# A first group that begins with its first tile: two sets of four PSUM banks, an earlier first weight piece, and a third context block turned inside head six

## The reference, cut to what matters

```python
    x = x + _L0_xattn_ref(ctx_2048, ctx_2048, _layernorm(x, axis=-1), L0_xattn_ssm_kernel, L0_xattn_D, 8)
    x = x + _L0_ffn_ref(_layernorm(x, axis=-1), L0_ffn_gate_w, L0_ffn_w_gate, L0_ffn_w_up, L0_ffn_w_down, L0_ffn_sw_gate, L0_ffn_sw_up, L0_ffn_sw_down)
    # _L0_xattn_ref
        kv = jnp.einsum('bhil,bhjl->bijhl', k_, v_)
        kv_f = jnp.fft.rfft(kv, n=fft_size)
        kernel_f = jnp.fft.rfft(ssm_kernel, n=fft_size)
        y = jnp.fft.irfft(kv_f * kernel_f, n=fft_size)[..., :L]
        out = y + kv * D[None, None, None, :, None]
        out = jnp.einsum('bijhl,bhil->bjhl', out, q_)
    # _L0_ffn_ref
        scores = jax.nn.softmax(x @ gate_w.T, axis=-1)
        topk_w, topk_i = jax.lax.top_k(scores, K)
        gact = jax.nn.silu(jnp.einsum('ech,ehi->eci', xg, w_gate))
        mid = gact * jnp.einsum('ech,ehi->eci', xg, w_up)
        eout = jnp.einsum('eci,eih->ech', mid, w_down) * wbuf[..., None]
        shared = jax.nn.silu(x @ sw_gate) * (x @ sw_up) @ sw_down
```

## Time and profile before

| | |
|---|---|
| median of 3 runs | 613.25 us (612.37 to 613.38) |
| the profiled execution | 613.41 us, span 611.3 us |
| PE busy | 591.2 us, 97% of the span |
| DVE, ACT, POOL busy | 485.8, 289.7, 407.4 us |
| mean granted TensorE clock | 0.994 |

### The profile page before, as it was taken

How to read it: one execution, slowest core, us unless ns; L and a number is a source line. 1 busy time by engine, 2 the same in 40 slices (tenths; PEclk the granted TensorE clock), 3 DMA queues, 4 the chain that set the end, 5 groups by cost and what they waited for, 6 DMA issues and landing times.

```text
span 611.3 us, 13710 instructions
## 1 busy us (share of the span) xinstructions
PE 591.2 (97%) x4411; PEld 552.7 (90%) x4411; DVE 485.8 (79%) x1279; ACT 289.7 (47%) x520; POOL 407.4 (67%) x499
## 2 busy tenths in 40 slices
PE   7989999999999999999999999999999999999993
PEld 7768989999999989999999898999999999999992
DVE  6999787679779689598699879999878888877730
ACT  3426334434435334345261344576556665656631
POOL 6988798778888789789771272187448886334242
PEclk9999999999999999999999999999999999999997
DMA  6665315226236145251340147698888889888443
GB/s 178 233 184 173 105 36 173 73 74 166 88 94 165 49 111 155 52 142 47 86 113 2 53 160 240 200 291 229 226 215 242 228 224 236 240 234 245 123 59 45
DMA packets 60238, 91.50 MB, mean 150 GB/s; under 512 B 4262, under 2 KB 36006, under 8 KB 60188
## 3 DMA queue, kind: packets, MB, share of 16 engines
q1 hardware_dynamic: 52912, 74.00, 39.9%
q0 software_dynamic: 7168, 16.78, 13.4%
q10 hardware_dynamic: 108, 0.08, 0.1%
HBM read 73.76 MB, written 17.09 MB: 149 GB/s over the span
## 4 chain that ended last, share of the span: by engine, by line
PE 82%; DVE 6%; POOL 4%; issue 4%; ACT 2%; DMA 1%; DVEq 1%; POOLq 0%; ACTq 0%
PE gu L684 19%; PE gu L843 14%; PE yb L562 11%; PE mb L860 10%; PE yb L843 7%; PE gu L722 7%; PE mb L534 4%; PE yb L614 3%; PE yb L534 2%; POOL kv L1257 1%; DVE prod L1521 1%; PE gu L763 1%; DVE prod L1523 1%; DVE oT L1541 1%; DMA xg<-normalised_tokens,slot_rows 1%
## 5 line engine op out<-in xcount | busy, mean ns | idle before, releaser
L684 PE MATMUL gu<-xT,sw 128*128 128x256 f32 (+2 forms) x1104 | 136.4, 281 | 0.0
L684 PEld LDWEIGHTS gu<-xT,sw 128*128 128x128 f32 (+2 forms) x1104 | 131.8, 180 | 0.5 <-issue 0.2
L1257 POOL TENSOR_TENSOR kv<-kT 128x256 f32 (+3 forms) x232 | 106.1, 496 | 0.0
L1274 POOL TENSOR_TENSOR kvl<-kv,kvh 128x1440 fp32r<-128x1440 f32 (+1 forms) x26 | 82.3, 3167 | 26.3 <-ACT kvh L971 26.0
L1521 DVE TENSOR_TENSOR prod<-yb,qT 128x64 f32<-128x64 f32 (+10 forms) x272 | 74.7, 285 | 17.4 <-PE yb L614 11.7
L1541 DVE TENSOR_REDUCE oT<-prod 128x256 f32<-128x2048 f32 x32 | 73.0, 2280 | 0.1
L971 ACT ACTIVATE kvh<-kv 128x1440 fp32r<-128x1440 f32 (+1 forms) x26 | 35.2, 1352 | 73.9 <-POOL kv L1264 37.4
L562 PE MATMUL yb<-kvh,tlast 128*128 128x288 f32 x280 | 66.1, 297 | 0.0
L1523 DVE TENSOR_TENSOR prod<-yb,qT 128x96 f32<-128x96 f32 (+10 forms) x238 | 64.2, 270 | 0.0
L860 PE MATMUL mb<-ed,midh 128*128 128x512 f32 x180 | 57.4, 400 | 0.0
L1817 DVE TENSOR_TENSOR ew<-raw_w,ew 128x704 fp32r<-128x704 f32 x64 | 55.1, 882 | 0.3 <-ACT ew L1119 0.3
(11 more groups left out here) (218 smaller groups left out, 1296.0 us busy)
## 6 DMA issues: line engine op xcount, KB each, us to landing
raw_w<-in_L_ffn_w_gate_dram SPq DMA_DIRECT2D x16, 704.0 KB, 7.0
raw_w<-in_L_ffn_w_up_dram SPq DMA_DIRECT2D x16, 704.0 KB, 8.6
raw_d<-in_L_ffn_w_down_dram SPq DMA_DIRECT2D x16, 512.0 KB, 4.3
tlast<-toeplitz_taps SPq DMA_DIRECT2D x20, 384.0 KB, 3.7
tstep<-tap_steps SPq DMA_DIRECT2D x20, 256.0 KB, 4.2
c_t<-in_ctx_dram SPq DMA_DIRECT2D x16, 256.0 KB, 5.3
x_t<-in_x_dram SPq DMA_DIRECT2D x16, 256.0 KB, 5.1
normalised_tokens<-xn SPq DMA_DIRECT2D x16, 256.0 KB, 2.9
```

Source lines behind the costliest of these rows:

```text
L684: last = pe.matmul(bank[0:m, u * GT:(u + 1) * GT], sw[:, c, a, col:col + m], xT[:, c, b, :], start=(c == 0 and (a, b) == PASSES[0]), stop= ...
L1257: last = pool.tensor_tensor(to[:, :, POFF[d]:POFF[d] + w], src[:, :, 0:w], src[:, :, d * B:HD * B], ALU.mult)
L1274: pool.tensor_tensor(kvl[:, s, 0:nb, :], kv[:, s, 0:nb, :], kvh[:, s, 0:nb, :].bitcast(fp32), ALU.subtract)\
```

## The change

- **First group by tiles.** The first context tile and the first x tile are loaded ahead of the second ones, with a semaphore each (`ctx_first`, `x_first`). Tile 0 is turned, normalised and multiplied first (`first_stats`, `inverse_tile`); heads 0 and 1 use tile 0 alone. The second queries are turned inside head 2 (`second_queries`). PE begins with 2 dummy products instead of 5, and has 5 and 1 later instead of 17.
- **Banks.** `gu` and `mb` become one tensor `other` of four banks. Heads 1 and 3 go to `other`, heads 0, 2 and 4 to `yb`. DVE multiplies heads 1, 2 and 4 whole instead of by halves.
- **Taps.** `tap_rows` is loaded by SP, `skip_t` is ACT's first transfer, SP stores `first_taps`. The split of the taps (`padhl`) and the tap steps (`steps_of`, `stephl`) move behind the first products on DVE; the rounding of `stephl` goes to ACT and its subtraction to POOL.
- **Weights.** ACT rounds piece 0 ahead of the second copied queries. POOL's order becomes piece 0, `stephl`, `pairs(4)`, `inverse_x(1)`, piece 2, `pairs(5)`, piece 1, `inverse_t(0)`, piece 3.
- **Head five.** The third context block (`prep_ctx(2)`) is turned in the middle of `convolve(5)`, into `gu`, ahead of group 0's normalised tokens, which go into `gu` too.

```diff
+        other = es.enter_context(nc.psum_tensor("other", [P, LB, 512], fp32))
+        gu, mb = other[:, 0:2, :], other[:, 2:LB, :]
...
-        BY_HALVES = (0, 1, 2, GH, GH + 1)
-        FIRST_POOL = 3
+        BY_HALVES = (0, GH + 1)
+        FIRST_POOL = 4
...
+        FIRST_HOMES = {1: ((other, 0), (other, 2)), 3: ((other, 0), (other, 2)), GH + 1: ((mb, 0), (yb, 0))}
...
# SP
-            load_group(0, parts="c")
-            load_group(0, parts="x")
-            sp.dma_start(gate_rows[:], gate_w).then_inc(gate_in, 16)
+            sp.dma_start(tap_rows[:], taps).then_inc(taps_in, 16)
+            sp.dma_start(c_t[:, 0, :], c_g[0, 0]).then_inc(ctx_first[0], 16)
+            sp.wait_ge(pad_whole, 1)
+            sp.dma_start(first_dram, pad[0:WHOLE, :]).then_inc(first_out, 16)
+            sp.dma_start(c_t[:, 1, :], c_g[0, 1]).then_inc(ctx_first[1], 16)
             sp.wait_ge(first_out, 16)
             load_first(0)
-            load_group(1, parts="x")
+            sp.dma_start(x_t[:, 0, 1, :], x_g[0, 1]).then_inc(x_first[1], 16)
             load_first(1)
             load_first(2)
+            sp.wait_ge(c_tr, TT)
+            load_group(1, parts="c")
             load_first(3)
+            load_group(1, parts="x")
...
# PE
+                    convolve(GH * g, 0)
+                    pe.wait_ge(d_mul, 4)
+                    prep_q(g)
+                    mixed_out(g - 1, g)
+
+                    def turn():
+                        prep_ctx(g + 1)
+                        pe.wait_ge(k_ev, TT * (g + 2))
+                        normalised(g - 1)
+
+                    convolve(GH * g + 1, 1, turn)
...
-            idle_products(5)
-            prep_ctx(0)
-            idle_products(17)
-            convolve(0, 0, {1: lambda: prep_q(0)})
+            idle_products(2)
+            prep_ctx(0, [0])
+            idle_products(5)
+            gate_turned()
+            prep_ctx(0, [1])
+            idle_products(1)
+            prep_q(0, [0])
+            convolve(0, 0)
+            convolve(1, 1)
...
+            convolve(2, 2, {LB - 1: second_queries})
             prep_ctx(1)
...
# POOL
             pairs(1, 0, 1)
+            inverse_tile(1, x_stat, x_pow, x_rs)
             pairs(2, 0, 2)
             pairs(3, 0, 3)
+            split_shared(0)
+            pool.wait_ge(steps_h, 1)
+            pool.tensor_tensor(stephl[:, 1, :, :], steps_of[:], stephl[:, 0, :, :].bitcast(fp32), ALU.subtract)\
+                .then_inc(steps_hl, 1)
             pairs(GH, 1, 0)
             inverse_x(1)
+            split_shared(2)
             pairs(GH + 1, 1, 1)
-            split_shared(0)
-            split_shared(2)
             split_shared(1)
+            inverse_t(0)
             first_steps()
...
# DVE
+            gate_low()
+            multiply(0, 0, 0, lambda: first_stats(1, x_stat))
+            add_up(0, 0, 0)
             prep_stats(1, [0])
-            multiply(0, 0, 0, lambda: prep_stats(1, [1]))
-            add_up(0, 0, 0)
             head(1, 0, 1)
-            gate_low()
+            prep_stats(1, [1])
             head(2, 0, 2)
```

More of the change, by code:

```diff
@@ L616, in convolve, with prep_ctx, prep_q @@
                 last.then_inc(conv, 1)
[L618 to L621, removed]
+            def prep_ctx(g, tiles=range(TT)):
+                if isinstance(g, int) and g == 0:
+                    pe.wait_ge(ctx_first[tiles[0]], 16)
+                else:
+                    pe.wait_ge(ctx_in, 32 * g)
+                if isinstance(g, int) and g == 2:
+                    pe.wait_ge(x1_ok, TT)
+                else:
+                    wait(pe, n_l, TT * (g - 1))
+                for t in tiles:
                     wait(pe, q_ev, TT * (g - 1) + t + 1)
-                    transposes(mb[:, t, :], lambda c: c_t[:, t, c * P:(c + 1) * P]).then_inc(c_tr, 1)
-            def prep_q(g):
+                    bank = gu if isinstance(g, int) and g == 2 else mb
+                    transposes(bank[:, t, :], lambda c: c_t[:, t, c * P:(c + 1) * P]).then_inc(c_tr, 1)
+            def prep_q(g, tiles=range(TT)):
                 wait(pe, lg_ok, g - 1)
-                for t in range(TT):
+                for t in tiles:
                     pe.wait_ge(x_nrm, TT * g + t + 1)
@@ L635, in mixed_out @@
                     pe.wait_ge(d_sum, GH * g + (t + 1) * GH // TT)
-                    last = transposes(mb[:, t, :], lambda c: oT[:, LB - 1 - c, t * P:(t + 1) * P])
+                    if isinstance(g, int) and g == 0:
+                        pe.wait_ge(d_mul, 4)
+                    last = transposes(turned(g)[:, t, :], lambda c: oT[:, LB - 1 - c, t * P:(t + 1) * P])
                     last.then_inc(o_tr, 1)
@@ L942, in norm_q @@
             def norm_q(g, tiles=range(TT)):
-                act.wait_ge(x_rs, g + 1)
+                if isinstance(g, int) and g == 0 and tiles[0] == 0:
+                    act.wait_ge(tile_rs, 1)
+                else:
+                    act.wait_ge(x_rs, g + 1)
                 for t in tiles:
@@ L961, in evacuate @@
                     tile = dst[:, bass.ds(g % 2, 1), :, t * P:(t + 1) * P].rearrange("p s c w -> p (s c) w")
-                    act.activation(tile, mb[:, t, :].rearrange("p (c w) -> p c w", c=LB), ACT.Copy).then_inc(signal, 1)
+                    bank = gu if isinstance(g, int) and g == 2 and dst is kT else mb
+                    act.activation(tile, bank[:, t, :].rearrange("p (c w) -> p c w", c=LB), ACT.Copy).then_inc(signal, 1)
             def round_kv(n, s):
@@ L1302, in first_steps @@
                 split_shared(3)
-                inverse_t(0)
                 pairs(GH + 2, 1, 2)
@@ L1346, in _ @@
                 if d == HD - 2:
-                    inverse_x(0)
+                    inverse_tile(0, tile_stat, tile_pow, tile_rs)
                 w = (HD - d) * B
@@ L1486, in prep_stats @@
             def prep_stats(g, tiles=range(TT)):
-                if isinstance(g, int) and g == 1:
-                    dve.wait_ge(x_more, 32)
-                else:
-                    dve.wait_ge(x_in, 32 * g if not isinstance(g, int) or g else 32)
+                dve.wait_ge(x_in, 32 * g)
                 wait(dve, x_rs, g)
@@ L1508, in multiply @@
                     dve.wait_ge(conv, n + 1)
-                dve.wait_ge(q_ev, TT * g + TT)
+                dve.wait_ge(q_ev, TT * g + (1 if isinstance(n, int) and hl < GH // TT else TT))
                 wait(dve, d_sum, n)
```

158 lines of the change are left out of this document (88 added, 70 removed).

## The result

The changed kernel takes 615.21 us (median of 19 runs, 614.13 to 618.15), the kernel before 612.78 in the same comparison (19 runs, 612.16 to 615.37): ratio 1.0035, 95% interval 1.0021 to 1.0049. It is slower by 0.35%, about 2.1 us; the forecast was 613.1 and no measurable change. The ratio is an estimate of its own over all executions and differs a little from the quotient of the medians. The profiled execution took 614.61 us with a span of 612.7, against 613.41 and 611.3.

A forecast was written before the change was run, and what follows sets the result against it. PE bounds everything behind the beginning, its start hanging on POOL; 3.33 - 1.07 - 0.40 - 2.06 = -0.2 us takes the profiled 613.41 to 613.2, given as a 613.1 median, range 611.7 to 614.9.

The forecast's parts named there:

- Heads 1, 2, 3 and one set of statistics (4.04 - 2.04 = 2.0): DVE from 22.3 to add_x(0): three times 5.43 plus 2.0 gives 40.6, so inverse_t(0) at 44.5, 1.07 earlier.
- The sum for POOL: POOL from inverse_t(0) to inverse_x(2): moved weight piece +3.33, earlier start -1.07, vanished waits -0.40 and -2.06, together -0.2 us.
- the lead survives: Faster rival: POOL's way is shorter, PE is 1.5 us earlier at down(0) and group 1's tokens; 611.7, chance 0.17.
- The rival of the clock: Slower rival: PE's clock stays low into head 0, its first three products cost up to 1.5 us more; 614.4, chance 0.19.
- the new wait of POOL ahead of the second tile's power: POOL at inverse_tile(1), near 17 us: later work starts 2.35 us later, at no cost, with 0.4 us of cover.
- a wait at `down(0)` for `midl`: PE at down(0): there at 82.6, remainder at 83.7, so a new wait of about 1.1 us takes back gate_up's 1.5 lead.
- the place where the result can be read: PE at group 1's tokens, 92.62: its gain or loss there is the whole kernel's; 0.2 us earlier was forecast.

The follow-up runs named there:

- e1_onecol: Changed kernel with the second x block's two two-column finishing tensor_scalars split into four of one column; 612.06 us against 613.36 for the kernel before, ratio 0.9987.
- h1_probes_within: e1_onecol plus four unread two-column tensor_scalars on DVE within heads 1 and 2; 618.48 us against 613.84 for the kernel before.
- g2_probes: e1_onecol plus three unread two-column tensor_scalars on DVE, behind add_up(0), head 1 and head 2; run once for its profile, no time given.
- f1_onecol_tokens: e1_onecol with low_mid(0, 5) and inverse_t(1) earlier on POOL, group 1 normalised ahead of head 10's rounding on ACT; 611.33 us against 613.36 before, ratio 0.9963.

## Why the prediction was wrong

- **The step that failed** is "Heads 1, 2, 3 and one set of statistics (4.04 - 2.04 = 2.0)". From 22.3 it should have led to 40.6. DVE was at head 1 sooner, at 21.21 (-1.09); the statistics behind head 1 took from 26.62 to 31.78, 5.16 instead of 2.0 (+3.16); the three heads and sums took 0.17 more than 16.29. That gives 42.84, and `inverse_t(0)` follows 3.57 us later, at 46.41 to the hundredth. Forecast was 44.5. Without the shut-out the same statistics take 1.34 (26.32 to 27.66 in `e1_onecol`).
- **A price taken from a row whose neighbour had changed.** The 2.0 holds the same instruction, at 17.95 in the kernel before, where it took 0.55 with POOL as busy:

  ```profile
  17.95 0.55 DVE L1476 TENSOR_SCALAR xnm<-xmv 128x2 f32<-128x2 f32 x1
  ```

  There it found its place between two products. I took its size as fixed, though it depends on what POOL does beside it.
- **The sum for POOL was right in form.** With the measured places it reads 3.33 + 0.84 - 0.40 - (2.06 - 0.18) = +1.89; measured are +1.80 at `inverse_x(2)` and +1.77 at the tokens. With those of `e1_onecol`: 3.33 - 2.70 - 0.40 - 1.88 = -1.65; measured -1.71 and -1.74.
- **The rival "the lead survives"** named its condition, head 0 a full microsecond earlier. It starts 0.5 to 1.3 us earlier than 11.8 (11.06, 11.30, 10.75, 10.54 in the first four profiles). The taps were stored at 4.49 and loaded from 6.06, 1.57 later, where I had taken 3.12 from the kernel before; about 5.0 us then passed to head 0, where I had taken 4.1. In `e1_onecol` the lead is there (1.74 us at the tokens). In the changed kernel the shut-out eats it.
- **The rival of the clock** had the wrong place. Into head 0 the clock is full. It falls later, behind a wait of PE that I had not forecast: 1.69 us at head 4 in two of the four profiled executions in which the instruction took 4.08 or 4.09. In the first comparison the medians differ by 2.4 us, the two profiled executions by 1.2, and this cost does not explain the rest: its 15 executions at a mean clock of 0.990 or more have a median of 615.21 too. That rest stays open. The step behind the wait for normalised tokens, 4.34 for 3.56, is of the same kind, and stays in `e1_onecol`.
- **Right were** the new wait of POOL ahead of the second tile's power, at no cost by itself (2.47 us, 16.20); a wait at `down(0)` for `midl` (0.41, forecast about 1.1), though by luck, for `gate_up` came 1.26 us later than before and not 1.5 earlier; and the place where the result can be read.

## What to carry to other kernels

Read what the other engine does beside a small VectorE instruction before you take its duration from another place: a two-column tensor_scalar took 0.15 to 5.24 us here, and the trace books the stall as its own time, with no releaser. Mostly it costs what is left of GpSimd's instruction in progress; now and then it costs several more. Where such an instruction stands on the path next to a long run of GpSimd work, the one-column form, or a place in a gap of GpSimd, is cheap insurance. And a step that is moved out of a wait is worth something only if the wait is really short by then: the weight piece left POOL idle for 3.42 us.

## What the hardware showed

- Of 94 two-column tensor_scalars that were held by a busy POOL, 86 ended within 0.05 us of the end of the one instruction in progress, after 0.23 to 2.04 us (the longest under a 2.67 us `kvl` at 90.67 in `h1_probes_within`). The others took 0.43, 0.55, 1.43, four times 4.08 or 4.09, and 5.24 us. These too ended within 0.1 us behind a boundary between two of POOL's instructions, the 1.43 and the 5.24 where POOL ran dry. What decides which boundary lets DVE in stays open.
- One column (0.14 to 0.16) was not held in any profile, under `stephl` and under pairs alike. The Trainium skill ("VectorE: DVE Perf Modes", What auto-detection actually checks) wants the outermost non-unit dimensions even or equal for the two-port mode; one column has no such dimension, and the runs agree. Whether that mode is the cause no run shows.
- A subtraction on DVE with both inputs in SBUF (32x512, at 20.52) took 1.07 us beside POOL's pairs; the same instruction took 0.68 at 11.78 in the kernel before, 0.4 less. POOL's product that began at 21.01, under it, took 1.11 instead of 0.66 (20.44 in `g2_probes`): here DVE got in at a boundary and POOL waited.
- After waits of PE of 2.3 to 2.7 us the granted clock was 0.57 to 0.98 over the next stretch in some executions and 1.00 in others of the same kernel (`f1_onecol_tokens` and its repetition); behind the waits of 1.2 us of the kernel before it stayed at 1.00.
